# 32-wide attention: value products of one pair of heads between the maxima and scores of the next

## The reference

```python
# layer 0: one key and value head for all query heads; the result is added to x
scores = einsum('bqhd,bkd->bhqk', Q, K) / sqrt(32)
out = einsum('bhqk,bkd->bqhd', softmax(scores), V)
# layer 1: 16 key and value heads; an output projection follows
scores = einsum('bthd,bshd->bhts', q, k) / sqrt(32)
ctx = einsum('bhts,bshd->bthd', softmax(scores), v)
```

## Time and profile before

| | |
|---|---|
| median of 3 runs | 2667.43 us (2664.07 to 2667.71) |
| the profiled execution | 2664.14 us, span 2662.4 us |
| TensorE, weight loads | 2442.9 us (92%), 1774.3 us (67%) |
| VectorE | 1741.1 us (65%) |
| ScalarE | 1193.4 us (45%) |
| POOL | 157.1 us (6%) |
| mean granted TensorE clock | 0.960 |

### The profile page before, as it was taken

One profiled execution on the slowest core, in us unless ns is written; L12 is line 12 of the kernel. 1 busy time (PEld: TensorE's weight loads), 2 busy tenths in 40 slices (PEclk: granted clock), 3 DMA queues, 4 the chain that ended last, 5 costly groups with the idle time before them and its releaser, 6 DMA issues. The chain is left out here.

```text
span 2662.4 us, 38864 instructions
## 1 busy us (share of the span) xinstructions
PE 2442.9 (92%) x11362; PEld 1774.3 (67%) x11362; DVE 1741.1 (65%) x3714; ACT 1193.4 (45%) x2330; POOL 157.1 (6%) x263
## 2 busy tenths in 40 slices
PE   7999989799999499899997799999999999999579
PEld 6555547677777377555546577777777777777357
DVE  6677777777886732566646567667676666766643
ACT  3566765333333322366652444444444444444221
POOL 0000000100000000100021101001010101000100
PEclk9999999899999799899998899999999999999789
DMA  5622200000000222433301100000000000000101
GB/s 171 186 70 65 63 1 1 0 1 0 0 0 1 68 106 108 133 95 91 90 9 32 32 5 16 12 8 12 9 14 8 16 4 16 9 3 0 41 1 64
DMA packets 71591, 103.78 MB, mean 39 GB/s; under 512 B 14587, under 2 KB 27643, under 8 KB 71387
## 3 DMA queue, kind: packets, MB, share of 16 engines
q1 hardware_dynamic: 71514, 102.82, 13.0%
HBM read 72.90 MB, written 29.88 MB: 39 GB/s over the span
## 5 line engine op out<-in xcount | busy, mean ns | idle before, releaser
L2959 DVE SCALAR_TENSOR_TENSOR x_res<-xa_out_bank,xa_den,x_res 128x512 f32 (+1 forms) x256 | 191.4, 748 | 155.6 <-PE xa_out_bank L2599 155.6
L589 DVE TENSOR_REDUCE l1s_mx<-l1s_max_bank 128x1 f32<-128x512 f32 x256 | 160.2, 678 | 95.1 <-PE l1s_max_bank L449 95.1
L2868 ACT ACTIVATE xa_pT_hi<-xa_t_bank 128x512 fp32r<-128x512 f32 x256 | 149.4, 597 | 125.0 <-PE xa_t_bank L2736 125.0
L589 DVE TENSOR_REDUCE l0s_mx<-l0s_max_bank 128x1 f32<-128x512 f32 x256 | 159.9, 678 | 58.8 <-PE l0s_max_bank L449 58.7
L2879 ACT ACTIVATE xa_prob<-xa_prob,xa_nmax 128x512 f32<-128x512 f32 x256 | 182.7, 716 | 30.0 <-DVE xa_nmax L2941 30.0
L2599 PE MATMUL xa_out_bank<-xa_o_w,xa_o_hi 128*128 128x512 f32 x512 | 173.4, 420 | 22.3 <-DVE x_res L2959 20.8
L2923 DVE TENSOR_TENSOR xa_pT_lo<-xa_t_bank,xa_pT_hi 128x512 fp32r<-128x512 f32 x256 | 175.7, 687 | 22.7 <-ACT xa_pT_hi L2868 18.6
L2941 DVE CUSTOM_DVE_ANT_0 xa_prob<-xa_s_bank,xa_mask_bias 128x512 f32<-128x512 f32 x256 | 171.1, 687 | 22.1 <-PE xa_s_bank L2599 13.3
L1991 DVE SCALAR_TENSOR_TENSOR ffn_yT<-ffn_y,ffn_ysc,ffn_yT 128x512 f32<-128x512 f32 x176 | 129.6, 748 | 50.4 <-PE ffn_y L1763 50.3
L2736 PE MATMUL xa_t_bank<-ident,xa_prob 128*128 128x128 f32 x1024 | 149.8, 274 | 0.1
L2736 PEld LDWEIGHTS xa_t_bank<-ident,xa_prob 128*128 128x128 f32 x1024 | 120.1, 140 | 39.8 <-issue 18.3
(11 more groups left out here) (466 smaller groups left out, 5876.7 us busy)
## 6 DMA issues: line engine op xcount, KB each, us to landing
l0s_q<-l_q SPq DMA_DIRECT2D x96, 128.0 KB, 2.4
l1s_q<-l_q SPq DMA_DIRECT2D x96, 128.0 KB, 3.1
l1s_k<-l_k SPq DMA_DIRECT2D x96, 128.0 KB, 3.5
l0s_k<-l_k SPq DMA_DIRECT2D x96, 64.0 KB, 2.5
x_res<-in_x_dram SPq DMA_DIRECT2D x4, 1024.0 KB, 9.4
l_q<-l_q_hi SPq DMA_DIRECT2D x16, 256.0 KB, 2.6
l_q<-l_q_lo SPq DMA_DIRECT2D x16, 256.0 KB, 3.2
l_q<-l1p_hi SPq DMA_DIRECT2D x16, 256.0 KB, 2.1
```

What stands on the lines that cost most here:

```text
L589: dve.tensor_reduce(self.mx[:, j // QT, j % QT:j % QT + 1], self.max_bank[(2 * s + j) % 3][:], AX.X, ALU.max)\
L2868: act.activation(pT_hi[:, kt % (QT - 1), :], t_bank[kt % 2][:], ACT.Copy).then_inc(pT_hi_done, 1)
L2959: dve.scalar_tensor_tensor(xt, out_bank[:], den[:, r, 2, q:q + 1], xt, ALU.mult, ALU.add)\
```

## The change

Nothing is computed otherwise; the order changes on TensorE and ScalarE, and `weighed` is counted per key tile.

- TensorE, step p: for each key tile kt, first `weigh` of p-1 for kt, then two times `maximum` of p+2 and `score` of p (k = 2 kt and 2 kt + 1). `turn` of p-2 stands after the four matmuls of kt = 0, `max_rows` of p+1 after those of kt = 2. After the last step come `weigh` of the last pair and the last two `turn`.
- ScalarE, step p: before the first exponential of key tiles 0, 1 and 2 it waits until the pair before is weighed for that key tile, since `pT` is written again; before that of key tile 3 stands `take_oT` of p-1. `rows` of p+1 comes after exponential 5, no longer after exponential 7.
- POOL waits for the same event by its new count.

```diff
@@ weigh
-        if kt == QT - 1:
-            last.then_inc(self.weighed, 1)
+        last.then_inc(self.weighed, 1)
@@ tensor, step
-            for k in range(8):
-                m(k)
-                self.score(pe, p, s, k)
-            if next_rows:
-                self.max_rows(pe, p + 1, (s + 1) % R)
             for kt in range(QT):
-                self.weigh(pe, p, s, kt)
-            if not self.early(p, 1):
-                self.turn(pe, p - 1)
+                if not self.early(p, 1):
+                    self.weigh(pe, p - 1, (s - 1) % R, kt)
+                for k in range(2 * kt, 2 * kt + 2):
+                    m(k)
+                    self.score(pe, p, s, k)
+                if kt == 0 and not self.early(p, 2):
+                    self.turn(pe, p - 2)
+                if kt == 2 and next_rows:
+                    self.max_rows(pe, p + 1, (s + 1) % R)
 
         self.rounds(pe, step)
-        self.turn(pe, self.NP - 1)
+        for kt in range(QT):
+            self.weigh(pe, self.NP - 1, (self.NP - 1) % R, kt)
+        for p in range(self.NP - 2, self.NP):
+            self.turn(pe, p)
@@ stage_values
-            reached(pool, self.weighed, p - 1)
+            reached(pool, self.weighed, QT * (p - 1))
@@ take_oT
-        act.wait_ge(self.weighed, p + 1)
+        act.wait_ge(self.weighed, QT * (p + 1))
@@ scalar, step
-            if not self.early(p, 1):
-                self.take_oT(act, p - 1)
             for k in range(8):
                 n, kt = k % 2, k // 2
+                if n == 0 and not self.early(p, 1):
+                    if kt == QT - 1:
+                        self.take_oT(act, p - 1)
+                    else:
+                        act.wait_ge(self.weighed, QT * (p - 1) + kt + 1)
                 act.wait_ge(self.scored, 8 * p + k + 1)
...
-            if not self.late(p, 1):
-                self.rows(act, p + 1, (s + 1) % self.R)
+                if k == 5 and not self.late(p, 1):
+                    self.rows(act, p + 1, (s + 1) % self.R)
```

## The result

| | before | after |
|---|---|---|
| median | 2667.36 us (4 runs) | 2738.91 us (4 runs, 2737.38 to 2739.84) |
| ratio to before | | 1.0271 (95% interval 1.0253 to 1.0288) |
| profiled execution, span | 2664.14, 2662.4 us | 2739.75, 2737.7 us |
| first attention, first value product to the last's end | 273.3 us | 311.1 us |
| second attention, the same | 269.6 us | 305.5 us |

A forecast was written before the change was run, and what follows sets the result against it. TensorE was taken to bound both attentions, with a 0.47 us hold by VectorE a pair. Pairs of 9.90 us, against 8.63 and 8.68, gave +71.5 us on 2664.1: 2735.6, put at 2737 (own range 2722 to 2750, wider 2702 to 2752).

The forecast's parts named there:

- Step 1: At the maxima in each pair, TensorE's hold by VectorE goes: gain 0.47 us a pair (0.52 in the first attention).
- Step 2: On TensorE, entering and leaving a block of value products costs 0.35 us; three more blocks a pair: 1.05 us.
- rival B: Blocks of four matmuls are entered and left free: a pair 9.07 us, total 2686 us; chance 0.05.
- Step 3: `max_rows` of p+1, right after maxima 4 and 5, waits for VectorE's normalise of p-2: hold 0.64 us.
- Step 4: ScalarE's row copies and bank copy before the next pair's first value product: hidden, with 0.16 us to spare.
- Step 5: `turn`, POOL's value staging, SP's loads, semaphore increments and VectorE's unpacking in the first attention: moved past at no cost.
- The sum: Pair 9.90 us against 8.63 and 8.68; second attention 305.4 us (+35.8), first 309.0 us (+35.7).
- The last two steps: First attention's two steps without maxima, with context-tile turns beside them: 9.7 and 9.3 us by estimate.
- A: Block price real, but normalise doesn't hold `max_rows`; ScalarE's chain holds 0.31 us, pair 9.57 us, total 2718; chance 0.09.
- C: As rival B, normalise early enough, ScalarE's copies 0.49 us apart: 8.15 to 8.5 us a pair, 2642; chance 0.05.
- D: Rule on weight loads: leaving a block costs nothing more, 2 x 93 added blocks x 0.11 us less: 2717; chance 0.03.
- E: More holds than seen: ScalarE's spare 0.16 us used up, then 0.2 us in each of 56 pairs: 2748; chance 0.08.

## Why the prediction was right, point by point

- *Step 1, the hold by VectorE goes.* Shown: inside a group maxima and scores follow each other in 0.23 to 0.24 us. Its worth fits too: the transposes alone in the middle bring 0.41 us a pair, the 0.47 us less some 0.05 for a block that is now left straight to a maximum.
- *Step 2, a block costs 0.35 us.* Shown three ways: two blocks fewer 0.70 us a pair, one block more 0.33 to 0.34 us, and 128-column products remove nearly all of it. The doubt noted in rival B, that the long block before might be a poor model for a short one, came to nothing: 1.01 and 0.34 us behind short blocks.
- *Step 3, the row maxima wait 0.64 us for the normalise.* Measured 0.67, and gone when the normalise comes one maximum earlier. Two terms were off and nearly cancel: VectorE began to read 0.54 us after the maximum and not 0.61, and TensorE went on 0.15 us after the normalise and not 0.06.
- *Step 4, ScalarE's chain is hidden with 0.16 us to spare.* Hidden it is, with 0.21 us from the copy's end to the block. But the 0.05 us for the handover, read behind a row maximum, was too small: it is 0.14 here, so 0.07 us are to spare. When the hold of step 3 went, this chain took its place with 0.32 us, where 0.31 was forecast; there too, an earlier start of the copies made up for the longer handover.
- *Step 5, moved past at nothing.* POOL's values are named for part of TensorE's idle time before blocks, but those blocks start in the free 0.32 to 0.34 us behind a score, and POOL had copied their values a pair earlier.
- *The sum.* A pair of the second attention is 9.90 us as forecast, and its four parts (2.59, 2.13, 3.04 and 2.14 us) are each within 0.02 us. The second attention took 305.5 us against 305.4, the first 311.1 against 309.0. In the first, 27 pairs are 9.92 to 9.95 us (1 us together). The next one is 10.31, where TensorE waits for maxima that VectorE reads late, behind statistics for a later stage (L784). The last two steps, put at 19.0 "by estimate", took 19.9.
- *The total.* That it missed by only 2 us (2737 and 2738.9) is partly luck. The sum gave +71.5 us between the profiled executions, and their spans differ by 75.3: 2.2 us more in the attentions, and 1.6 behind them, where the sum has nothing. The kernel before has its median 3.2 us above its profiled execution, the changed one 0.8 us below.
- *The rivals.* A was realised by the experiment with the earlier normalise: 2719.7 where A said 2718. B and C are refuted by the block's price, and C also by ScalarE's row copies, which keep 0.6 us apart. (B's sum is also off: without the price of four blocks, less the 0.11 us that the hold of step 3 covers, the pair would be shorter by 1.29 us and not 1.10, and B some 10 us lower.) D took 0.11 us off each block; measured were the full 0.33 to 0.35, and the load behind value products is late only when the width changes. E's extra holds at the start of a pair are not there: every regular pair of the second attention is 9.90 us.

## What to carry to other kernels

Before interleaving two kinds of matmul to hide a wait, look at what a change between them costs in the trace: place where one ends and the other begins, measured start to start against the pace inside each. Here it was 0.35 us for each change from 128 columns to paired 64-column products and back, against a hold of 0.47 us, so that one more block a pair did no better than break even (2664.4 and 2665.2 us) and three more cost 71.5 us. To give a lagging engine time, put other work of the same shape (here the transposes) into the middle of the run; and when a step is moved forward, recompute what it waits for on every engine's own order, since the old slack (0.3 us here) does not move with it.

## What the runs showed of the hardware that was not expected

- The price of a change of width doesn't depend on how long the block is, as far as the three lengths here go. Blocks of 4, 8 and 16 matmuls take 1.01, 1.86 and 3.58 us to the next maximum: 0.85 for two more starts and 1.72 for four more, the bare 0.43 us a start, over the same 0.15 us.
- With 128-column products between maxima and scores the price is gone: entering in 0.24 us, and 1.10 us instead of 1.34 from the block to the score behind it.
- ScalarE's copies of 2 rows by 512 take 0.59 us each and start 0.61 us apart (1267.09 and 1267.70 in the changed kernel), while a copy of 128 rows takes 0.60. They don't overlap as its exponentials do (eight in 4.26 us), and they are part of what ended last in two of the experiments.
- How soon TensorE goes on after another engine is not one number: 0.05 us after a row maximum was read the earlier trace rows, but 0.15 after the normalise, 0.14 after the bank copy and 0.13 after the row copies. Where 0.2 us are to spare, that decides.
